# Running the input projection over four image quarters at once instead of two and two

## What is computed

```python
x = x + _L0_conv_ref(_gn(x), ...)   # six experts of two depthwise 3x3 convolutions, gated per image
x = x + _L1_conv_ref(_gn(x), ...)   # the block that this change touches

def _forward(x, w_in, dw_k, fft_filter, w_out):      # _L1_conv_ref
    x = jnp.einsum('oc,bchw->bohw', w_in, x)         # 32 -> 170 channels
    xf = jnp.fft.rfft2(patches_8x8(x)) * fft_filter  # a filter per channel on 8x8 patches
    x = unpatch(jnp.fft.irfft2(xf, s=(P, P)))
    y = depthwise_conv3x3(x, dw_k)
    g = jax.nn.gelu(y[:, :85], approximate=False) * y[:, 85:]
    return jnp.einsum('oc,bchw->bohw', w_out, g)     # 85 -> 32 channels
```

## Time and profile before

| What | us |
|---|---|
| median of 3 runs | 3460.51 |
| lowest and highest run | 3444.41, 3466.08 |
| span of the profiled execution (first to last instruction) | 3457.4 |

### The profile page before, as it was taken

How to read it: one execution, slowest core, us unless ns; L and a number is a source line. 1 busy time by engine, 2 the same in 40 slices (tenths; PEclk the granted TensorE clock), 3 DMA queues, 4 the chain that set the end, 5 groups by cost and what they waited for, 6 DMA issues and landing times.

```text
span 3457.4 us, 164388 instructions
## 1 busy us (share of the span) xinstructions
PE 2908.9 (84%) x74374; PEld 2020.6 (58%) x74374; DVE 1847.5 (53%) x4198; ACT 1311.5 (38%) x2217; POOL 253.1 (7%) x274
## 2 busy tenths in 40 slices
PE   4699999999996788888888888888888888888887
PEld 4355554555453666666666666666656666666665
DVE  3356565565652245554556555655555555555555
ACT  1234444444342233343434343433433333443332
POOL 2011111111110200000000000000000000000000
PEclk9899999999998599999999999999998999999999
DMA  6578778787764334334443444334433444334433
GB/s 126 124 170 172 164 169 170 172 171 165 165 144 69 32 100 111 95 93 104 117 106 89 107 119 105 89 99 105 116 97 89 105 115 112 89 99 113 113 92 84
DMA packets 451958, 404.16 MB, mean 117 GB/s; under 512 B 404172, under 2 KB 404478, under 8 KB 447497
## 3 DMA queue, kind: packets, MB, share of 16 engines
q1 hardware_dynamic: 446030, 376.93, 47.5%
q10 hardware_dynamic: 5228, 16.70, 1.4%
HBM read 165.77 MB, written 78.16 MB: 71 GB/s over the span
## 4 chain that ended last, share of the span: by engine, by line
PE 49%; DVE 6%; issue 5%; ACT 3%; DMA 3%; ACTq 2%; SPq 1%; POOL 0%; DVEq 0%; POOLq 0%
PE ps L1295 12%; PE ps L1245 10%; PE ps L1280 10%; PE ps L1309 9%; PE ps L1263 8%; DMA neighbours<-border 3%; DVE gated L1356 3%; ACT gelu L1180 2%; DVE channels_first L1369 2%; ACTq L1190 2%; ACT hidden_patches L1153 1%; DVE border L1163 1%; SPq L1052 1%; ACT border L1163 0%; DMA x_normed<-in_L_conv_w_in_dram 0%
## 5 line engine op out<-in xcount | busy, mean ns | idle before, releaser
L1356 DVE TENSOR_TENSOR gated<-gelu,ps 128x432 f32<-128x432 f32 (+1 forms) x512 | 289.3, 567 | 555.8 <-ACT gelu L1180 529.7
L449 ACT ACTIVATE hidden<-ps,hidden_scale 128x576 f32<-128x576 f32 x512 | 351.7, 738 | 614.5 <-PE ps L554 614.5
L1369 DVE STREAM_TRANSPOSE channels_first<-gated 128x512 f32<-128x512 f32 x576 | 571.3, 1043 | 1.1
L1153 ACT COPY hidden_patches<-ps 128x704 f32<-128x704 f32 x576 | 406.5, 749 | 434.3 <-PE ps L1245 434.2
L1280 PE MATMUL ps<-hidden_patches,channel_tables 64*64 64x144 f32 x11264 | 403.4, 287 | 97.4 <-DVE gated L1356 97.4
L1263 PE MATMUL ps<-hidden_patches,channel_tables 64*64 64x144 f32 x11264 | 405.7, 287 | 90.2 <-DVE border L1163 84.8
L568 PE MATMUL ps<-hidden,taps 128*32 128x288 f32 x6144 | 437.3, 417 | 43.1 <-DMA taps<-conv_tables 29.7
L1245 PE MATMUL ps<-w_in_t,x_normed 32*64 32x88 f32 x18432 | 422.3, 259 | 54.2 <-issue 49.3
L1263 PEld LDWEIGHTS ps<-hidden_patches,channel_tables 64*64 64x64 f32 x11264 | 359.4, 134 | 184.6 <-ACT border L1163 114.7
L1163 ACT COPY border<-ps 128x432 f32<-128x432 f32 (+1 forms) x512 | 226.4, 495 | 618.9 <-DVE border L1163 216.9
L554 PE MATMUL ps<-x_rows,taps 32*64 32x288 f32 x12288 | 455.0, 415 | 2.5 <-issue 1.3
(11 more groups left out here) (147 smaller groups left out, 1328.7 us busy)
## 6 DMA issues: line engine op xcount, KB each, us to landing
neighbours<-border SPq DMA_DIRECT2D x1024, 126.8 KB
taps<-conv_tables SPq DMA_DIRECT2D x192, 216.0 KB
x_image<-in_x_dram SPq DMA_DIRECT2D x128, 288.0 KB, 5.8
x<-x_image SPq DMA_DIRECT2D x128, 288.0 KB, 4.7
x_image<-x SPq DMA_DIRECT2D x384, 96.0 KB
out_dram<-x_image SPq DMA_DIRECT2D x384, 96.0 KB, 2.0
x_rows<-in_x_dram SPq DMA_DIRECT2D x512, 60.0 KB
neighbours<-border ACTq DMA_DIRECT2D x1024, 15.8 KB
```

Of the source, the lines that this page charges most:

```text
L449: A(hid[T % 3][:, 2 * h:2 * h + 2, :, 1:1 + W], ps1[:, 2 * h:2 * h + 2, 0:XB * W].rearrange("p c (k w) -> p c k w", k=XB), ACT.Relu, scale ...
L1153: nc.scalar.copy(o, i).then_inc(s_we[pair], 1)
L1356: TT(o, gl[odd][:, 0:n * NPC].rearrange("p (t m) -> p t m", m=NPC), ps[:, 2 * odd + 1, 0:n * NPC].rearrange("p (t m) -> p t m", m=NPC), AL ...
L1369: last = nc.vector.transpose(t[:, s], g)
```

## The change

`w_in_step` loses its argument `pair`. It waits for both pairs' copies of the step before, then issues the step's matmuls patch by patch over all four quarters. `s_w` is still raised twice: by the last matmul of quarter 1 and by the last of quarter 3, both in the last patch. The number of matmuls, their operands, the banks, ScalarE's copies and the order of all other engines stay as they were. Lines after the function move down by one or two.

```diff
--- before.py
+++ after.py
@@ -1231,20 +1231,22 @@
                                   mid[half(h), j:j + n, NCH * g:NCH * g + NCH], start=True, stop=True)
                     last.then_inc(s_x, 1)
 
-            def w_in_step(k, v, pair):
-
-                if v == 0 and pair == 0:
+            def w_in_step(k, v):
+
+                if v == 0:
                     pe.wait_ge(s_xn, k + 1)
-                need(pe, s_we[pair], NW * k + v)
-                if k == 0 and v == 0:
-                    pe.wait_ge(s_xe[pair], NGX)
+                for pair in range(2):
+                    need(pe, s_we[pair], NW * k + v)
+                    if k == 0 and v == 0:
+                        pe.wait_ge(s_xe[pair], NGX)
                 for i in range(WSTEP):
-                    for q in (2 * pair, 2 * pair + 1):
+                    for q in range(NQUAD):
                         cq = slice(C * q, C * q + C)
                         for h in range(2):
                             last = MM(ps[half(h), 4 + q, i * NCH:(i + 1) * NCH], xn[cq, (WSTEP * v + i) * NV:(WSTEP * v + i + 1) * NV], wi[cq, NCH * h:NCH * h + NCH],
                                       start=True, stop=True)
-                last.then_inc(s_w, 1)
+                        if i == WSTEP - 1 and q % 2 == 1:
+                            last.then_inc(s_w, 1)
 
             def border(S):
 
@@ -1314,8 +1316,7 @@
             for k in range(B + 1):
                 for v in range(NW):
                     if k < B:
-                        w_in_step(k, v, 0)
-                        w_in_step(k, v, 1)
+                        w_in_step(k, v)
                     if k > 0:
                         w_out_step(k - 1, v)
                 if k < B:
```

## The result

The changed kernel takes 3489.32 us, median of 4 runs (3476.54 to 3507.22), against 3457.55 us for the kernel before in the same session (4 runs). The ratio is 1.012, 95% interval [1.0071, 1.0169]. The quotient of the two medians is 1.0092, 31.8 us. The ratios of this document are those on record with their intervals; the quotients of the medians differ from them by up to 0.003, inside the intervals. So the change makes the kernel slower by about 1%, where 3454, slightly faster, was forecast; the time lies inside the range that the prediction gave.

The account below looks back on a forecast made before the run. The prediction took TensorE's instruction supply, 2.84 us a step, and low-clock stretches to bound the stages. Full-clock steps +6, 0.50-clock steps -18 and image 0 +6 gave -6: 3451 us profiled, 3454 as forecast; range 3425 to 3515.

Parts of the forecast that it names:

- The supply: TensorE in image 9's stage: instructions arrive at 128 matmuls per 3.78 us, so a full-clock step costs 2.84, not 2.18.
- missing record: Image 9's stage: 127 matmuls counted between the first two stops, taken as 128 if the profile lacks one record.
- Steps at full clock, images 1 to 31: Stages of images 1 to 31: waits for copies replace stops for instructions; 0.2 us an image, +6 (0 to +47).
- the hand-over of 0.05: From the copies' end to the next w_in: 0.05 us in the 2.49 loop, after 0.04 seen in image 0's stage.
- The loop: A full-clock step: w_in 1.05, both copies 1.39, hand-over 0.05, together 2.49 us (2.34 to 2.74) instead of 2.18.
- The time by that rule, +77: If instruction fetch is hidden, every step goes from 2.18 to 2.49: 0.31 x 248 = +77, about 3540 us.
- Steps at the 0.50 clock, -18: Low-clock steps of images 1 to 31: shorter w_in takes a step from 3.91 to 3.29 us; -18 (-23 to 0).
- Image 0, +6: Image 0's stage, w_in alone: each of 9 steps takes on the second copy, 0.64 us; +6, up to +19 more.
- The stops are no supply limit: Rival, chance 0.20: at the next w_in's wait, fixed stops per 128 matmuls add to the 2.49 us step; 3515 us.
- The low stretches vanish: Rival, chance 0.15: shorter w_in keeps the clock up, stages of images 1 to 31 take 25.7, not 27.2; 3426 us.
- the clock stays low: Rival, chance 0.06: waiting for copies keeps most stages at 0.50, a step costs 3.29 instead of 2.84; about 3570 us.

Follow-up runs that it names:

- one wait: The changed kernel with w_in's head waiting for pair 1's copy alone instead of both pairs' copies; 3432.6 us, 0.9966 of the kernel before.
- swapped waits: The changed kernel with the two waits at w_in's head in the other order, pair 1's copy named first; 3447.77 us, 1.0013 of the kernel before.

## Why the prediction was wrong

*The supply.* The reading of rows 6 was half right. The stops are not fixed mishaps: where TensorE lost time without a further instruction that only waits, they shrank (one wait: 49.3 to 31.0 us, stages at full clock 25.7 as before). But "128 matmuls per 3.78 us, however fast it could run them" is not so. About 1.2 of the 3.78 us is TensorE's own way from a stop to the next packet. What holds TensorE's issue in that part makes the whole interval longer; what holds it later is hidden by the 2.5. And the rows' count held a sign of the waits: the 127 matmuls between the first two stops, with as many weight loads, are 254 instructions, and w_out's two waits between them, each an instruction of its own, make 256. The prediction's missing record isn't needed.

*The step that failed* is the term "Steps at full clock, images 1 to 31", +6 with the ends 0 and +47. It took the waits for copies as covered by the stops. The stages with the clock at 1.00 grew by 27.2 - 25.7 = 1.5 us, the term's upper end, instead of 0.2: 31 x 1.5 = +46 where +6 stood, and with it the forecast gain became a loss. The range had that end, for a loop without cover, so it held the time; the forecast's mechanism did not. Two sentences ahead of it let it: "No instruction is added or removed", which holds for the operations but not for the program, and the hand-over of 0.05 taken from rows 9, which have one wait at that place. Two waits on one instruction became an instruction and a wait, and the one that ends last was in the slow position.

*The sum by the runs.* The changed kernel against the swapped waits: 0.0107 x 3443 = 37 us (with the room told above). The step without a stop is 2.50 to 2.52 instead of 2.42; 0.08 for each of 168 + 19 waits for copies makes 15. The packet after a stop in w_out is 1.74 - 1.30 = 0.44 later, at 40 stops, 18. So 33 of 37 is accounted for; this working is an estimate from one profiled execution of each. The swapped waits against one wait: 0.0047, 16 us; 0.14 later at 40 stops is 6 of it, and 10 stay open (the intervals leave room for about that). One wait against before: -0.0034, -12 us. Together 37 + 16 - 12 = 41, which is the 1.2% by the ratio; the medians have 32.

*The copies.* The loop was right: w_in takes 1.00 to its copies' start 0.96 later (1837.48 to 1838.44), and a step 2.50 to 2.52 where 2.49 was forecast. The Trainium skill, "TensorEngine Tiling (Array Packing)", section "PSUM Bottleneck", says that after a fourfold speedup of TensorE by tiling the copy out of PSUM may become the bottleneck. In the steps without a stop the trace shows such a bottleneck at a far smaller speedup (w_in's row of 64 from 1.24 to 1.00): 168 waits for the copies in place of 8. Yet the kernel with one wait and the same copies is faster than before, so the bottleneck in a step didn't decide the time.

*The fetch.* The Trainium skill, "Runtime: NRT & Kernel Launch", section "Instruction fetch mechanics", calls the fetch hidden. The prediction set that aside by rows 6, and the runs agree with the rows: 31.0 us of stops at w_in even with one wait, and 2.5 to 2.6 us from packet to stop's end in each kernel of the table. The time by that rule, +77, would have been too high.

*Steps at the 0.50 clock, -18.* The direction was right. w_in at 0.50 takes 1.46 to the start of w_out, forecast 1.42, before 2.04:

```profile
1902.14 1.50 PE L1311 MATMUL ps<-channels_first,w_out_t 128*32 128x128 f32 x32 [2.13 <-DVE channels_first L1370]
1903.57 1.53 PE L1246 MATMUL ps<-w_in_t,x_normed 32*64 32x88 f32 x64
1905.03 1.55 PE L1311 MATMUL ps<-channels_first,w_out_t 128*32 128x128 f32 x32
```

And the time at 0.50 fell from 144 to 88 us. One profile each doesn't tell how much of this is the order's; other profiles here have 36 to 152. The clocks of all runs tell more: on average 0.960 in the 84 runs of the kernel before beside the experiments and 0.959 to 0.962 in the three experiments that keep its order of matmuls, but 0.964 to 0.968 in each of the nine kernels that mix the pairs. So the new order does raise the clock, by about 0.006. At 14 us per 0.01 that is some 8 us, an estimate, and less than half of the 18. Why the clock rises, the runs don't show.

*Image 0, +6.* Right: 27.4 - 21.6 = +5.8.

*The rivals.* "The stops are no supply limit" gave 3515 and came nearer on the time: intervals beyond 3.9 decide it, as the prediction said, and image 9 shows 4.15 on average. But its mechanism, a stop that stays whatever comes, is not what the runs show; the kernel with one wait has shorter stops. That its figure came nearer is in part luck, since it also left out the clock's gain. "The low stretches vanish" and "the clock stays low" did not happen.

## What to carry to other kernels

Count the waits at the head of a group of matmuls in the built program, not in the code. Each beyond the first is an instruction of its own that TensorE's issue goes through. Leave out those that another wait implies, and of two that are needed let the one that is met first be the instruction of its own; here the wait that the code writes last becomes it. An engine that stops for instructions at even intervals is not a fixed supply behind which other waits hide; ask in which part of the interval the new wait falls.

## What the runs showed that was not expected

Swapping the order in which two waits are written, without any other edit, took the ratio from 1.012 to 1.0013. Leaving out one wait per step that never decides anything made the kernel before 0.5% faster. And instruction packets start when TensorE has got some 1.2 us past a stop, with the block needed about 2.5 us after its packet starts. What ties the packet to TensorE's progress, the trace shows only by these times. That it is the number of instructions issued is a reading, and no run here changed that number alone.
